# Twelve of the sixteen attention batches in a loop on every engine, in an attention and mixture-of-experts kernel

## The reference

```
x = x + layernorm(attention(layernorm(x)))
x = x + layernorm(experts(layernorm(x)))
attention: q, k, v = x Wq, x Wk, x Wv        16 heads of 64
           causal softmax(q k^T / 8) v, then Wo, + its input, layernorm * gamma + beta
experts:   softmax router over 8 experts, the best 2 of each row;
           out = sum of gate * (gelu(x w1[e]) w2[e]),  w1[e] 128x512, w2[e] 512x128
```

## Time and profile before

| | us |
|---|---|
| median of three runs | 815.32 (814.24 to 819.53) |
| the profiled execution | 813.7 |
| its span | 811.9 |
| one batch in the attention | 36.45 to 36.48 |
| PE busy over the span | 757.3 (93%) |

### The profile page before, as it was taken

One profiled execution on the slowest core, in us unless ns is written; L12 is line 12 of the kernel. 1 busy time (PEld: TensorE's weight loads), 2 busy tenths in 40 slices (PEclk: granted clock), 3 DMA queues, 4 the chain that ended last, 5 costly groups with the idle time before them and its releaser, 6 DMA issues.

```text
span 811.9 us, 19170 instructions
## 1 busy us (share of the span) xinstructions
PE 757.3 (93%) x5936; PEld 615.6 (76%) x5937; DVE 622.6 (77%) x2357; ACT 526.4 (65%) x1739; POOL 266.9 (33%) x397
## 2 busy tenths in 40 slices
PE   4999999999999999999999999999978999999965
PEld 3777777777878787777778787777757878888941
DVE  4668888888888888888888888888878775555526
ACT  4676767777676777777676777777655534444415
POOL 3004434133231323133231313233115554344425
PEclk9999999999999999999999999999999999999978
DMA  8420000000000000000000000000011232112146
GB/s 195 133 51 8 8 10 20 14 22 18 11 21 8 21 11 18 15 21 18 11 21 9 21 15 16 14 15 18 5 35 44 68 93 61 59 59 59 56 146 185
DMA packets 51623, 33.14 MB, mean 41 GB/s; under 512 B 10960, under 2 KB 48336, under 8 KB 51536
## 3 DMA queue, kind: packets, MB, share of 16 engines
q1 hardware_dynamic: 46608, 22.73, 10.6%
q0 software_dynamic: 4352, 9.05, 3.1%
q10 hardware_dynamic: 576, 0.27, 0.1%
HBM read 19.81 MB, written 12.22 MB: 39 GB/s over the span
## 4 chain that ended last, share of the span: by engine, by line
PE 83%; DVE 6%; ACT 4%; issue 3%; DMA 2%; DVEq 1%; SPq 0%; ACTq 0%; POOL 0%; POOLq 0%
PE PT1O L411 12%; PE SC L397 9%; PE M L376 7%; PE A L417 6%; PE M L378 5%; PE M L377 5%; PE SC L403 5%; PE PT L574 4%; PE A L585 3%; PE SC L585 3%; PE SC L400 3%; PE PT L424 3%; PE PT1O L428 3%; PE PT L425 3%; PE SC L376 2%
## 5 line engine op out<-in xcount | busy, mean ns | idle before, releaser
L1057 ACT ACTIVATE qk<-M 128x512 f32<-128x512 f32 x128 | 76.5, 598 | 156.2 <-PE M L378 156.2
L1063 ACT ACTIVATE prob<-SC,nmax 128x256 f32<-128x256 f32 x256 | 126.0, 492 | 0.0
L411 PE MATMUL PT1O<-pT,v_sb 128*64 128x256 f32 (+1 forms) x1024 | 111.7, 339 | 9.6 <-issue 6.4
L695 DVE TENSOR_SCALAR prob<-prob,rden 128x256 f32<-128x256 f32 x256 | 101.6, 397 | 9.0
L1061 ACT ACTIVATE prob<-SC,nmax 128x128 f32<-128x128 f32 x256 | 97.0, 379 | 0.0
L411 PEld LDWEIGHTS PT1O<-pT,v_sb 128*64 128x64 f32 x1024 | 64.2, 136 | 42.3 <-ACT pT L1068 7.0
L1270 POOL DMA_INDIRECT expert_rows<-v_sb,got x72 | 69.1, 960 | 82.1 <-ACT v_sb L1146 76.8
L397 PE MATMUL SC<-qk 64*128 64x256 f32 x512 | 90.5, 430 | 0.8 <-ACT qk L1057 0.8
L1001 DVE COPY hidT<-PT 128x512 f32<-128x512 f32 x72 | 49.7, 691 | 49.5 <-PE PT L574 47.6
L1263 POOL DMA_INDIRECT sent_rows<-rec,slot x64 | 63.7, 995 | 72.6 <-DVE slot L851 54.5
L689 DVE TENSOR_REDUCE nmax<-SC 128x2 f32<-128x512 f32 x128 | 87.1, 680 | 0.0
(11 more groups left out here) (182 smaller groups left out, 1841.8 us busy)
## 6 DMA issues: line engine op xcount, KB each, us to landing
got<-sent_rows SPq DMA_DIRECT2D x72, 66.0 KB, 1.8
w_in<-expert_rows SPq DMA_DIRECT2D x16, 256.0 KB, 3.7
x_in<-L_attn_x SPq DMA_DIRECT2D x16, 128.0 KB, 2.1
w_in<-L_ffn_w SPq DMA_DIRECT2D x1, 2048.0 KB, 12.1
x_res<-L_attn_x SPq DMA_DIRECT2D x16, 128.0 KB, 2.1
w_sb<-L_ffn_w SPq DMA_DIRECT2D x8, 256.0 KB, 4.3
out<-y_out SPq DMA_DIRECT2D x8, 256.0 KB, 2.3
expert_rows<-v_sb,got POOLq DMA_INDIRECT x72
```

The costliest lines, as they stand in the source:

```text
L411: last = mm(O[k * E:(k + 1) * E, cols], v_sb[:, t, h * E:(h + 1) * E], src[:, k, :], start=(t == 0), stop=(t == 1), skip_group_check=True)
L695: v.tensor_scalar(prob[:, par, k, P:3 * P], prob[:, par, k, P:3 * P], rden[:, par, k:k + 1], None, ALU.mult)
L1063: a.activation(prob[:, par, k, P:3 * P], SC[par][:, k, LATE_Q], ACT.Exp, bias=nmax[:, par, k:k + 1], accum_out=den[:, par, k:k + 1]).then_ ...
```

## The change

`over_batches` calls the body with numbers for b = 0, 1, 2, then once inside a loop (`Fori`) whose register runs over 3 to 14, then with numbers again for 15, 16 and 17. This holds for all five engines. The work of each batch and its order on each engine stay as they are. On GpSimd one more semaphore increment stands ahead of the copy of the residual.

```
             def run(eng):
-                for b in range(B + LAG):
+                for b in range(LAG + 1):
+                    body(b)
+                with eng.Fori(LAG + 1, B - 1) as b:
+                    body(b)
+                for b in range(B - 1, B + LAG):
                     body(b)
             return run
...
                 if not is_last(b):
                     pool.wait_ge(sem("att_done"), b + 1)
+                    q.sem_inc(sem("residual_turn"), 1)
                     q.tensor_copy(xn_res[:], xn[:]).then_inc(sem("xn_kept"), 1)
```

## The result

The changed kernel takes 818.88 us (median of 20 runs, 816.32 to 820.85) against 816.18 us of the kernel before on the same chip (20 runs, 813.69 to 819.53): ratio 1.0032, 95% interval 1.0021 to 1.0044. That is 2.7 us slower, a third of a per cent, and within the 1% that counts as no change. A second measurement in a later session gave 1.0021 (1.0006 to 1.0036).

A forecast was written before the change was run, and what follows sets the result against it. PE, busy for 93% of the span, was taken to bound the kernel. Two waits moved onto register instructions add 1.9 us, all other terms 0: 815.3 + 1.9 = 817 us, no change; range 812.5 to 830 us.

The forecast's parts named there:

- Waits against registers: In the loop on every engine: register instructions with engine work queued ahead, nearly all of those added, cost 0.
- Two carried waits: Steps 2 and 5: a register addition carries PE's wait for qk_sb before transposes; 0.08 us each, 1.9 us total.
- The branch back: Behind step 7's transposes on PE: 0.49 us hidden by 0.85 us of cover, so 0; upper end 5.4 us.
- Fetching the instructions: Loop return on every engine: bodies stay at hand, so no packet is loaded again; 0 us.
- the first rival: Loop return on DVE or ACT: packets fetched each time, 11.6 us in all (829 us) or 34 (851 us); chance 0.13.
- The sequencers fall behind: PE's 25 register instructions exposed: 829 us at 40 ns, 865 at 0.16 us; only DVE's in step 6: 820; chance 0.08.
- faster by POOL's shift: Step 6: POOL's residual sum moves, PE wins its 0.05 and 0.2 us waits; 3 us gained, 812 us; chance 0.06.
- Theory C: From the experiments: the loss lies behind the attention, SP or POOL leaving loops or starting tiles late; about 1 us.

The follow-up runs named there:

- the first four experiments: Against the kernel before (824.39 us): loop on TensorE alone 1.0010; loops on all but TensorE 0.9986; all loops with four more carried waits 1.0059; two waits swapped 1.0011.

## Why the prediction was right, point by point

**Waits against registers: 0.** Right. Outside the two places nothing in the changed kernel's loop comes over 0.03 us later, and with loops on the four other engines alone nothing is lost (0.9986 and 0.9981).

**Two carried waits: 0.16 us per batch, 1.9 us in all, with ends at 0 and 3.9.** Right in mechanism, place and size: 0.07 us each, 1.7 us over twelve batches if nothing is won back, and 1.6 us from batch 3 to batch 15 (1.0 us in the repeat). Six such waits and half of one kind gave the loss in proportion. The price was the middle between 0 and a third of the tile loop's return, and came out 0.01 us off. That it came so near is luck: no row showed this form, so another value between 0 and 0.16 us would have been as well founded.

**The branch back: 0.** Right for this kernel: 0.27 us of idle behind it, the same as in the kernel before. The cover was even larger than the 0.85 us read from PE's own rows, because the sequencer is ahead of the engine: 1.35 us lie between the branch's end and the weight load, and 1.2 us of each fetch were hidden. Still it is less robust than that promises. With the waits swapped, 0.43 us appear near six of eleven returns, and I can't say why.

**Fetching the instructions: 0; the first rival.** Right: no packet in the loop. The bodies kept are those of 657 and 1312 instructions on PE, of 180 and 356 on DVE and up to 367 on ACT; those of 1967 on PE and 532 on DVE were fetched anew at each return, and 488 on ACT stopped it as well. This settles the point that the trace of before could not. The Trainium skill ("Runtime: NRT & Kernel Launch", "Instruction fetch mechanics") gives 2048 and 512 instructions and speaks of two blocks. The runs here come near its sizes, but bodies somewhat under them (1967 and 488) already stop their engines. That would follow if room is given in whole packets, of which such a body touches one more than its length asks for, but this was not measured. The prediction also said that by two blocks of q14's size DVE and ACT would fetch at every return. This doesn't follow from its own count of two packets for each body, unless one of the two blocks is always taken by what comes next. No fetch was seen, and 356 instructions on DVE, more than two packets of 128, stayed too. The rival's price for DVE, 2.0 us of fetch less 0.95 us of cover, is about what the kernel with three batches on DVE then paid: 1.9 to 2.2 us, 0.74 to 1.00 us of it on the path. Only its threshold was elsewhere.

**The sequencers fall behind; faster by POOL's shift.** Neither came. POOL's residual sum did meet another division (the first of L701 in step 6, 0.76 us where 0.28 is usual, and no longer the one of the earlier trace rows), and PE won nothing by it: no loop batch of the changed kernel is under 36.5 us.

**The sum and the median.** 817 us were forecast, 818.88 measured. Of the 1.9 us between them, 0.9 is the base: the kernel before had 816.18 us over twenty runs, not 815.3. The change itself was put at 1.9 us and measured at 2.7, of which the loop has 1.6. The other 1.1 us lie behind the loop, where the prediction has no term. Two things were seen there, and neither is shown to be the change's doing.

The first is the clock. The period behind the loop goes with how long the clock was granted at its lower level between 605 and 625 us: 36.2 us with no such stretch (both runs with straight text on PE), 36.8 to 37.4 with 3.4 us of it (the kernel before and five others), 37.9 to 38.6 with 6.8 us (the changed kernel twice, the loop on PE alone, four more waits, four batches per iteration), 39.5 with 10.2 us (three batches on DVE). By the profiles alone the changed kernel has the longer stretch. But most runs have their mean granted clock on record, and these don't bear it out: beside each other on one chip, the changed kernel has 0.987 (12 runs) and the kernel before 0.986 (23 runs). On the chip of the first four experiments, the kernel before has 0.984 and 0.983 in two sessions, the loop on PE alone 0.984, and the versions with loops on the four other engines, where PE doesn't fetch, 0.985 to 0.987. So the longer stretch isn't shown for more than the executions that were profiled, and loops on the other engines rather go with more of the clock. Why is open. The part of the gain of straight text on PE that its batches don't explain goes with it.

The second is the wait for gathered rows in the tiles, 0.9 us before and 2.2 us after. Over all fourteen profiles it lies between 0.4 and 2.2 us, and the time behind the period has no order by version. On the chip of the first four experiments it is 197.8 us with the loop on PE alone, 197.7 and 198.4 us with straight text on it, and 197.9 to 199.3 us in the others. What is left behind the loop is not steady either. By the medians it is 1.1 us in the first measurement, 0.9 us in the repeat, and less than nothing (-0.5 us) with the loop on PE alone. Theory C is excluded for SP and POOL by the version with straight text on PE; what the whole change may cost behind the loop stays open, at about 1 us at most by these medians.

## What to carry to other kernels

What this loop costs is what its register instructions put between a late signal and the matmul that needs it: look for waits that end idle time on the bounding engine, and whether a value is computed behind them. Having no value to compute there took the 0.07 us away (two batches per iteration); putting the waits in another order did too, but lost more elsewhere, so measure such a remedy by the whole loop. Then count the body on each engine against what stays resident, and ask what covers a fetch there. The engines that aren't the bound could be looped for nothing here: straight text on TensorE and loops on the others has the lowest ratio, though within a quarter of a per cent of the kernel before.

## What the runs showed of the hardware

- A wait that sits on a register addition of PE's sequencer delays the matmul behind it by 0.07 us (0.34 for 0.27 us idle), measured at two, six and, in half of the batches, one place per batch.
- Bodies that stay resident: up to 1312 instructions on PE, 356 on DVE and 367 on ACT. Not so with 1967, 532 and 488. A fetch at the return stops PE for 2.7 to 3.8 us and DVE, where it fetches alone, for 1.9 to 2.2 us. Behind six of the eight stops of PE (three and four batches per iteration) the clock fell to 1.2 GHz for 3.4 us, which costs a batch about 1.5 us more.
- At the return PE's sequencer is 1.35 us ahead of the engine. This hides the branch's 0.2 us, and 1.2 us of a fetch.
- The length of PE's pause doesn't decide alone whether the clock falls. It fell behind a stop of 2.74 us (three batches on PE) and stayed behind one of 3.34 us (three on all engines). And at the end of the attention, the kernel before and the one with straight text on PE have nearly the same 5 us ahead of 604.8, and then part. The kernel before:

```profile
599.84:604.84 5.00, 2.34 (x20) 1.55 (x18) 2.82 (x16) 3.04 (x10) 0.00 (x0) 1.00 0.32 75
604.84:609.84 5.00, 3.96 (x18) 2.80 (x18) 1.55 (x7) 1.26 (x3) 2.54 (x4) 0.66 0.04 14
```

And the version with straight text on PE (its second run), where the clock stays at 1.00:

```profile
599.79:604.79 5.00, 2.45 (x20) 1.54 (x18) 3.01 (x17) 3.03 (x10) 0.00 (x0) 1.00 0.27 69
604.79:609.79 5.00, 3.51 (x23) 2.65 (x24) 1.93 (x8) 1.47 (x3) 2.89 (x4) 1.00 0.04 14
```

PE did 23 matmuls there in 3.51 us and 18 in 3.96 us of busy time in the other. What decided it is open.
- The records of PE's matmuls can hide a stop: their ends are modelled, and ACT's start (0.87 us behind a weight load in place of 0.43) told of the 0.43 us.
